# Loads issued by scan block, z placed up to a tile sooner with a second copy of x, and the LayerNorm sums of second feed-forward rows ahead of the delta step

## What is computed

```
x = x + 0.5 * ffn(layernorm(x))
x = x + attn(layernorm(x))
x = x + 0.5 * ffn(layernorm(x))

ffn:  vecs = einsum('arh,bsh->bsar', A, x)          # 64 experts of 16
      idx  = top 4 of norm(vecs) over the experts
      out  = x W^T + bias + sum over chosen a of B[a] (mean of chosen vecs)
attn: xz = x W_xproj^T;  delta_r, B, C = split(xz)
      delta = softplus(delta_r W_dt^T + b_dt)
      h_t = exp(delta A) * h_(t-1) + delta * B_t * x_t       # 1024 channels, 16 states
      y_t = sum over states of h_t * C_t;  out = y + x * D
```

## Time and profile before

| | us |
|---|---|
| median of three runs | 2799.12 |
| lowest, highest | 2798.25, 2800.99 |
| the profiled execution, its time | 2797.06 |
| the profiled execution, span of its instructions | 2795.3 |
| PE, POOL, DVE, ACT busy in it | 2602.9, 2348.2, 2220.1, 1496.2 |

### The profile page before, as it was taken

How to read it: one execution, slowest core, us unless ns; L and a number is a source line. 1 busy time by engine, 2 the same in 40 slices (tenths; PEclk the granted TensorE clock), 3 DMA queues, 4 the chain that set the end, 5 groups by cost and what they waited for, 6 DMA issues and landing times.

```text
span 2795.3 us, 39869 instructions
## 1 busy us (share of the span) xinstructions
PE 2602.9 (93%) x13664; PEld 1176.9 (42%) x13664; DVE 2220.1 (79%) x2933; ACT 1496.2 (54%) x3363; POOL 2348.2 (84%) x703
## 2 busy tenths in 40 slices
PE   4989999999999999999999999999999999989999
PEld 1444444444344443444444434444444443434444
DVE  8447888888888887888878888788888888888843
ACT  5346666665555655556555555565555554655521
POOL 2138889989899898998999989999899999989910
PEclk8999999999999999999999999999999999999999
DMA  5144544544354443644544445444455434454321
GB/s 219 48 116 137 144 127 131 161 142 139 109 164 140 135 138 112 163 140 127 147 143 132 144 137 163 138 126 129 151 153 158 143 119 141 136 145 145 91 58 53
DMA packets 303520, 373.50 MB, mean 134 GB/s; under 512 B 148435, under 2 KB 220243, under 8 KB 303318
## 3 DMA queue, kind: packets, MB, share of 16 engines
q1 hardware_dynamic: 286422, 337.40, 40.5%
q10 hardware_dynamic: 16896, 33.56, 4.1%
HBM read 234.05 MB, written 103.29 MB: 121 GB/s over the span
## 4 chain that ended last, share of the span: by engine, by line
PE 22%; DVE 19%; DVEq 5%; ACT 4%; DMA 4%; issue 4%; POOL 2%; SPq 1%; ACTq 1%; POOLq 0%
DVE mreg L1147 10%; PE pv L554 7%; PE po L554 5%; PE pv L558 3%; PE po L558 3%; PE py L721 2%; ACT pA L934 2%; DMA delta_scratch<-mreg 2%; DVE pv L1108 1%; DVE sel L1105 1%; DVEq L1113 1%; DMA mreg<-xnT_scratch 1%; DVEq L1107 1%; DVEq L1063 1%; DVE sel L1116 1%
## 5 line engine op out<-in xcount | busy, mean ns | idle before, releaser
L522 POOL TENSOR_TENSOR mreg<-mreg 128x2048 f32<-128x2048 f32 x256 | 1160.9, 4535 | 37.9 <-ACT hst L920 37.8
L1147 DVE TENSOR_TENSOR_SCAN mreg<-pA,hst,mreg 128x512 f32<-128x512 f32 (+1 forms) x1024 | 1042.9, 1065 | 98.9 <-ACT pA L934 70.0
L934 ACT ACTIVATE pA<-mreg,nA 128x512 f32<-128x512 f32 (+1 forms) x1280 | 739.0, 596 | 465.9 <-DVE mreg L1147 413.2
L512 POOL TENSOR_TENSOR mreg<-mreg 128x1024 f32<-128x1024 f32 x340 | 795.3, 2363 | 226.3 <-DMA mreg<-delta_scratch 219.6
L554 PE MATMUL pv<-wA,xT 128*128 128x512 f16 x2016 | 463.2, 382 | 40.5 <-DVE xT L1085 23.8
L554 PE MATMUL po<-wB,uT 128*128 128x512 f16 x2016 | 472.1, 381 | 13.5 <-DVE xin L1071 10.2
L554 PE MATMUL po<-wW,xT 128*128 128x512 f16 x2016 | 470.1, 380 | 0.0
L506 POOL TENSOR_TENSOR mreg<-mreg 128x2048 f32<-128x2048 f32 x86 | 389.7, 4532 | 1.4 <-issue 1.4
L554 PEld LDWEIGHTS pv<-wA,xT 128*128 128x128 f16 x2016 | 191.4, 98 | 323.1 <-ACT xT L841 60.3
L554 PEld LDWEIGHTS po<-wB,uT 128*128 128x128 f16 x2016 | 192.1, 98 | 277.9 <-issue 49.4
L554 PEld LDWEIGHTS po<-wW,xT 128*128 128x128 f16 x2016 | 196.0, 98 | 238.3 <-issue 24.6
(11 more groups left out here) (132 smaller groups left out, 2404.1 us busy)
## 6 DMA issues: line engine op xcount, KB each, us to landing
mreg<-delta_scratch SPq DMA_DIRECT2D x256, 512.0 KB, 6.0
delta_scratch<-mreg ACTq DMA_DIRECT2D x128, 256.0 KB
xin<-x SPq DMA_DIRECT2D x32, 512.0 KB, 3.7
x_scratch<-xin SPq DMA_DIRECT2D x32, 512.0 KB, 6.7
xnT_scratch<-auxs SPq DMA_DIRECT2D x32, 512.0 KB, 2.9
mreg<-xnT_scratch SPq DMA_DIRECT2D x64, 256.0 KB, 6.6
yT_scratch<-mreg SPq DMA_DIRECT2D x64, 256.0 KB, 2.5
uT<-yT_scratch SPq DMA_DIRECT2D x32, 512.0 KB, 4.7
```

Of the source, the lines that this page charges most:

```text
L512: pool.tensor_tensor(h[:, half * n:half * n + n, :], u, b.broadcast_to([P, n, c.width]), ALU.mult).then_inc(s_bm, 1)
L522: pool.tensor_tensor(h, h, by_c, ALU.mult).then_inc(s_cm, 1)
L934: last = nc.scalar.activation(dst[:, part, :], src[:, part, :], ACT.Exp, scale=nA[:, m:m + 1])
L1147: last = V.tensor_tensor_scan(h, split(pA[:, i % 2, :], c)[:, part, :], h, before, ALU.mult, ALU.add)
```

## The change

Four things, in `plan`, in SyncE's program and in VectorE's:

- **Loads by block.** `slot` is gone. `loads(a, lo, hi)` walks over the scan blocks of a stretch of the unit, in twentieths as `scans` does, and issues at fixed blocks of a tile: the input spreads of the next tile at blocks 6 and 7, the y store and the first delta spread at 9, the second delta spread at 15. B and C stand at the first block of their group.
- **Two copies of x.** Of the three `xt` buffers two now serve the delta step alone and come free when DVE's delta operation has read them (`s_du`). The third serves `sum_up`: `load_again` loads the same tile a second time at block 13 of its own scan, once the y tile before it is stored, and `sum_up` also waits for that load (`s_ldv`). It is 64 more DMAs of 256 KB.
- **z sooner.** With `AHEAD = 10` the delta step of tile t stands at group 4t - 10 at the latest, at first places (position 0) wherever the rule allows; before, it stood at group 4t - 6, at either position. The x tile for position 0 is loaded at the end of the unit before, behind the store of its result; the first of a chunk has its rank load there too.
- **LayerNorm sums.** Where `b` is of kind 2, `unit_stats(b)` stands before `delta(a, 0)` and `scans(7, 10)`; before, it stood behind them. For kind 1 it stays.

```diff
@@ plan
+        ready_at = f1_at[first_tile[t].row1 - 1] + 2 if t in first_tile else 0
+        late_u, late_i = slot_unit[max(4 * t - AHEAD, 0)]
+        at = (max(prev[0] + 1, ready_at), 0)
+        if at > (late_u + (late_i > 0), 0) and prev[1] == 0 and prev[0] >= ready_at:
+            at = (prev[0], 1)
@@ SyncE
             def load_tile(t):
                 sp.wait_ge(s_stn, 16 * chunk_of_tile[t].row1)
-                sp.wait_ge(s_sty[t % NXT], 16 * (t // NXT))
+                sp.wait_ge(s_du, max(t - NXT + 2, 0))
+            def load_again(t):
+                sp.wait_ge(s_sty, 16 * t)
+                sp.dma_start(tile_of(NXT - 1, t), blocks_of(xnT_u, t)).then_inc(s_ldv, 16)
+            def loads(a, lo, hi):
+                for i in range(block_at(a, lo), block_at(a, hi)):
+                    t, n = i // 16, i % 16
+                    if n == 6 and t + 1 < NTL:
+                        spread_inputs(t + 1, 0)
+                    if n == 7 and t + 1 < NTL:
+                        spread_inputs(t + 1, 1)
+                    if n == 9 and t >= 1:
+                        store_tile(t - 1)
+                    if n == 9 and t + 1 < NTL:
+                        spread_delta(t + 1, 0)
+                    if n == 13 and t < NTL:
+                        load_again(t)
+                    if n == 15 and t + 1 < NTL:
+                        spread_delta(t + 1, 1)
...
@@ SyncE's unit
-                slot(a, 0)
-                if 0 in a.zs:
-                    load_tile(a.zs[0])
-                    ranks_due(a, 1)
+                ranks_due(a, 1)
+                loads(a, 0, 2)
...
+                loads(a, 2, 9)
...
+                loads(a, 9, 18)
...
+                loads(a, 18, 20)
+                if b and 0 in b.zs:
+                    ranks_due(b, 0)
+                    load_tile(b.zs[0])
@@ VectorE
             def sum_up(t):
                 dve.wait_ge(s_e, 4 * t + 4)
+                dve.wait_ge(s_ldv, 16 * (t + 1))
@@ VectorE's unit
                 scans(5, 7)
+                if b and b.kind == 2:
+                    unit_stats(b)
                 delta(a, 0)
                 scans(7, 10)
-                if b:
+                if b and b.kind == 1:
                     unit_stats(b)
```

More of the change, by code:

```diff
@@ L12 @@
 NXT = 3
+AHEAD = 10
 LEAD = 14
@@ L95, in plan @@
     for t in range(NTL):
-        s = 4 * t - 6
-        u, i = slot_unit[s] if s >= 0 else (SCAN0 - 1, 3)
-        at = (SCAN0 - 1, 2) if t == 0 else (u, 0) if i == 0 else (u, 1) if i < 3 else (u + 1, 0)
-        assert at > prev, (t, at, prev)
-        if t in first_tile:
-            f = f1_at[first_tile[t].row1 - 1]
-            assert at[0] >= f + 2 or (at[0] == f + 1 and at[1] == 2), (t, at, f)
+        ready_at = f1_at[first_tile[t].row1 - 1] + 2 if t in first_tile else 0
[3 more added lines that the diff above has]
+            at = (prev[0], 1)
+        if t == 0:
+            at = (SCAN0 - 1, 2)
+            assert f1_at[first_tile[0].row1 - 1] + 1 == at[0]
+        elif t > 2:
+            u, i = slot_unit[4 * t - 6]
+            assert at <= ((u, 0) if i == 0 else (u, 1) if i < 3 else (u + 1, 0)), (t, at)
         us[at[0]].zs[at[1]] = t
@@ L267, in build @@
         s_ldb = [sem(f"s_ldb{n}") for n in range(4)]; s_ldc = [sem(f"s_ldc{n}") for n in range(4)]
-        s_ldt = [sem(f"s_ldt{n}") for n in range(NXT)]; s_sty = [sem(f"s_sty{n}") for n in range(NXT)]
+        s_ldt = [sem(f"s_ldt{n}") for n in range(NXT - 1)]; s_ldv = sem("s_ldv"); s_sty = sem("s_sty")
         s_ldd = [sem(f"s_ldd{n}") for n in range(NPR)]; s_ldu = [sem(f"s_ldu{n}") for n in range(NPR)]
@@ L283, in column, with by_part @@
             return 16 * (channels_at(i // 16) + part) + i % 16
-        def rows_of(t):
-            return xt[:, t % NXT, :].rearrange("p (u k t) -> p k u t", k=chunk_of_tile[t].parts, t=P)
+        def by_part(slot, t):
+            return xt[:, slot, :].rearrange("p (u k t) -> p k u t", k=chunk_of_tile[t].parts, t=P)
         def split(a, c):
             return a.rearrange("p (k t) -> p k t", t=c.width)
-        def slot_of(a, n):
-            return a.slots[n] if n < len(a.slots) else None
         def block_at(a, twentieths):
@@ L331, in load_y @@
                     sp.wait_ge(s_out, a.u * 2 + 2)
-                    for n in range(NXT):
-                        sp.wait_ge(s_sty[n], 16 * len(range(n, chunk_of_row[b.v].tile1, NXT)))
+                    sp.wait_ge(s_sty, 16 * chunk_of_row[b.v].tile1)
                     src = yT_d[row:row + P, :].rearrange("p (k t) -> p k t", t=P)
@@ L403, in turn @@
                     sp.dma_start_transpose(uT[:, part, :, :], src).then_inc(s_uc[part], 16)
-            def slot(a, n):
-                G = slot_of(a, n)
-                if G is None:
+            def loads(a, lo, hi):
+                if a.u < SCAN0 or a.u > SCAN1:
                     return
-                t = G // 4 + 1
-                if G % 4 == 2:
-                    if t >= 2:
-                        store_tile(t - 2)
-                    if t < NGRP // 4:
-                        spread_inputs(t, 0)
-                        spread_inputs(t, 1)
-                        spread_delta(t, 0)
-                if G % 4 == 3 and t < NGRP // 4:
-                    spread_delta(t, 1)
-                for c in CH[1:]:
-                    if c.group0 - 4 <= G < c.group0:
-                        spread_b(c, G - c.group0 + 4)
-                    if c.group0 - 2 <= G < c.group0 + 2:
-                        spread_c(c, G - c.group0 + 2)
+                for i in range(block_at(a, lo), block_at(a, hi)):
[12 more added lines that the diff above has]
+                        spread_delta(t + 1, 1)
+                    for c in CH[1:]:
+                        if n % 4 == 0 and c.group0 - 4 <= i // 4 < c.group0:
+                            spread_b(c, i // 4 - c.group0 + 4)
+                        if n % 4 == 0 and c.group0 - 2 <= i // 4 < c.group0 + 2:
+                            spread_c(c, i // 4 - c.group0 + 2)
             def ranks_due(a, pos):
@@ L431, in unit @@
                 late = l if l and l.kind == 1 else None
-                if 0 not in a.zs:
-                    ranks_due(a, 1)
-                slot(a, 0)
-                if 0 in a.zs:
-                    load_tile(a.zs[0])
-                    ranks_due(a, 1)
+                ranks_due(a, 1)
+                loads(a, 0, 2)
                 if b:
@@ L1129, in delta @@
                 dve.drain()
-                dve.wait_ge(s_ldt[t % NXT], 16 * (t // NXT + 1))
+                slot = t % (NXT - 1)
+                dve.wait_ge(s_ldt[slot], 16 * (t // (NXT - 1) + 1))
                 c = chunk_of_tile[t]
```

19 lines of the change are left out of this document (7 added, 12 removed).

## The result

The changed kernel takes 2840.35 us, the median of four runs (2835.88 to 2846.36), beside 2800.05 us for the kernel before on the same chip. The ratio is 1.0146, with a 95% interval of 1.0127 to 1.0166: 40.3 us slower, where 27 us faster was forecast. The profiled execution took 2835.88 us and has a span of 2834.1 us.

The account below looks back on a forecast made before the run. PE was taken as the bound, with 1 to 2 us of rest a unit. One sum gave 29.9 us less, another 15.3; 27 was taken: 2770 us profiled, 2772 us median, range 2746 to 2798.

Parts of the forecast that it names:

- the new waits of SP: SyncE's queue: block-7 input spread waits for POOL, hidden with some 4 us to spare; rank load behind result's store, free.
- DVE's six waits and PE's six: DVE's waits for x tiles (23.6 us) and PE's for ACT's last delta copy (13.2 us) would go.
- the five old doubles: Units with a second delta step, 12, 20, 28, 44 and 52: their excess of 17.5 us would go.
- POOL's 112.3 us: POOL's waits for spreads would go nearly all; only the 8.2 us pushed onto PE counted.
- The 7 us charged for moving 22 delta steps: DVE: delta steps moved ahead of three scans and `prepare` cost 0 to 1.4 us in ten units; half taken.
- The reason given: ACT still does a decay needing the last scan ahead of `prepare`: 0.7 us later in 28 units, 19.6 us lost.
- the ring: DVE's work ahead of ACT's `prepare`, then PE: sets a unit's length where PE idles, 1.23 us in unit 42.
- The first sum: Three stages rebuilt from quiet units' times: 390.8, 1451.6 and 522.4 us, together 29.9 us less, 2767.2 us.
- the healing: Disturbed units would run like quiet ones, including a dozen that lie 1 to 3 us above them.
- The new wait of SP: Rival: POOL ends the block-7 product late, delaying transposes and input load in seven units, 21 us: 2793 us; chance 0.12.
- The slower case: Rival: moved delta steps cost 1.4 us in all 22 units and doubles keep their stall: 2815 us; chance 0.12.

Follow-up runs that it names:

- e3_spread13: Changed kernel with the second delta spread issued at block 13, ahead of the second load of x, instead of block 15: 2787.94 us, 0.9964 of the kernel before.
- e2_sums_back: Changed kernel with the LayerNorm sums back behind the three scans: 2823.7 us, 1.0092 of the kernel before.
- e5_behind_reload: As e4_both, but the second delta spread at block 13 stands behind the second load of x, not ahead of it: 2781.89 us.
- e6_z_late: As e4_both, but z stands at its old place, six groups ahead of its tile instead of ten: 2776.68 us.
- e4_both: Changed kernel with the LayerNorm sums back and the second delta spread at block 13, ahead of the second load of x: 2761.96 us, 0.9871 of the kernel before.
- e10_prepare_first: As e3_spread13, but on ACT the preparation and normalized input of a next unit of kind 2 go ahead of two decays: 2811.78 us.
- e11_inputs9: As e4_both, but the second input spread is issued at block 9, ahead of the y store, instead of block 7: 2764.62 us.

## Why the prediction was wrong

**Loads by block: the step that failed.** The prediction counted this part as a gain alone. It checked the new waits of SP (the block-7 input spread, the rank load) and the spreads ahead of the transposes, and did not ask of each spread when it is *wanted*. The second delta spread is read first by the decay of block 2 of the next tile, which may run once block 0 of that tile is scanned. From the start of block 15 to there are two blocks, 4.7 us at 18 blocks in 42 us, and a spread takes 5.3 us to land. So it arrives in time only where SP runs ahead of the engines. From its issue to the end of that block 0, the spread has less time than it then takes to land in 30 of 63 tiles of the changed kernel, and in 4 of the kernel before (from the timelines of SyncE and DVE). Of the two delta spreads it is the one with less room, and it went from the slot of a tile's fourth group (blocks 12 to 15) to block 15, in the units 10, 18, ... 58 directly behind the two transposes, and everywhere behind the second load of x. The cost is 52.4 us in the changed kernel (e3_spread13), 61.7 us without the moved sums; of the latter, 41.8 are the block (e2_sums_back against e5_behind_reload) and 19.9 the place behind the second load. With this one line at block 13 the direction of the forecast is right (e3_spread13, 0.9964).

**Second copy of x: right in its mechanism, wrong in one cost.** DVE's six waits and PE's six are gone, and the five old doubles went from 227.5 to 213.6 us, 13.9 of the 17.5 expected. The 64 reloads were costed at nothing since "nothing waits for a reload". Nothing does, but a spread queues behind one: e5_behind_reload puts 19.9 us on that order. These are part of the 61.7 us, since in the change the second load stands ahead of the spread too.

**z sooner: right, and understated.** POOL's 112.3 us went to 3.1. The 7 us charged for moving 22 delta steps do not show as a loss in e6_z_late, where z's old place costs 14.7 us. This is a net figure; the cost of the moved steps by itself was not measured.

**LayerNorm sums: right.** 19.6 us forecast, 19.1 (alone in the kernel before), 16.7 (in the change) and 26.0 (e3_spread13 against e4_both) measured. PE's wait for the normalized input in an undisturbed unit 42 was to be 1.9 us; in e3_spread13 it is

```profile
1898.28 0.66 PE L552 MATMUL pv<-idf,xn 128*128 128x128 f32 x4 [1.90 <-ACT xn L842]
```

The reason given was only half of it. The late decay ahead of `prepare` is real, but e10_prepare_first shows that with that decay out of the way the ring closes through the next one.

**The first sum, tested by e4_both.** Without the moved sums it gives 390.8, 1440.4 and 514.0 us for the three stages. Measured in e4_both:

```profile
223.40:620.10 396.70, 379.26 (x2204) 183.06 (x2219) 336.75 (x510) 257.68 (x647) 371.31 (x110) 1.00 0.50 148
620.10:2067.10 1447.00, 1391.12 (x7091) 613.44 (x7124) 1220.19 (x1457) 812.05 (x1734) 1386.98 (x409) 1.00 0.50 149
2067.10:2587.40 520.30, 489.35 (x2660) 219.17 (x2671) 443.21 (x627) 287.83 (x666) 490.79 (x145) 0.99 0.48 144
```

2364.0 us against 2345.2, 6 us too low in each stage: the healing was taken as complete, and e4_both still has ACT waits (16.2 us) and bunched loads. Which of these makes the 18.8 us is not shown. The total of e4_both is off by less (2762.0 against 2772 - 19.6 = 2752.4) in part by luck: unit 4 begins 5.8 us sooner (223.4 instead of 229.2), which no part of the prediction counted, and the forecast had been put 2.9 us above the first sum. The gap from 2772 to 2840.4 us is thus 52.4 us for the late spread, 6.4 us more for the sums beside an early spread (26.0 for 19.6), and these 9.6 us: 68.4 us.

**The rivals.** The new wait of SP (2793) was the right queue and the wrong wait: e11_inputs9 takes 144 us of SP's hold behind POOL away and wins nothing. The slower case (2815) had the right sign and a mechanism, the delta steps on the ring, that is not what happened: e4_both has all of z's moved steps and is 36.5 us faster than before. The range ended at 2798 because the one cost that mattered had been put at zero with no upper bound. "A DMA that is issued later" should have been bounded by its own landing time (5.3 us) times the tiles in which its room is gone. The seven units in which it meets the transposes give 37 us by this, an estimate that would have told the sign, though it is under the 52.4 us measured.

## What to carry to other kernels

In a queue that is held by waits, a place is an order, not a time: for each load that a change moves, write down which instruction reads it first, how long it takes to land, and which waiting DMAs stand between; the one with least room decides. Put a load that an engine waits for ahead of those that only free or refill something. When a bundle of edits goes wrong, move its single lines: here one line was worth 52 us, and the same bundle with this line moved and the sums left where they were runs in 2762 us instead of 2840.

## What was not expected of the hardware

- A 512 KB spread that SyncE issues within 3 us behind one of ScalarE's stores of the delta step lands in 8.4 us (median of 33 in e4_both), the others in 4.9 us, with the DMA engines about half busy. Why is open.
- A wait of ACT for a spread went with 0.83 to 1.09 us of the whole time for each us in five pairs of runs, though ACT is busy for 53% of the span only; the last 10.3 us of it were worth 1.8. PE's lower clock after the stall takes part in this: 0.93 granted in unit 34, and eight matmuls at 3.16 us instead of 1.90.
- SyncE's longest wait was harmless: 409.1 us in 51 places for POOL in e4_both, and with 144 us of it taken away the time stayed as it was, and SyncE stood longer at other waits. The sum of a queue's waits said nothing of their price.
